# A Mamba block and a mixture of experts on one core: the engine loop written out, and the gate product of y in two halves

## What is computed

```python
u, res = split(layernorm(x) @ W_in);  u = silu(u)
delta = softplus(u @ W_delta + b_delta);  Bm = u @ W_B;  Cm = u @ W_C
h_t = exp(delta_t * A) * h_{t-1} + delta_t * B_t * u_t      # 256 channels, 16 states
y_t = sum_n h_t[n] * C_t[n]
x = x + ((y + u * D) * silu(res)) @ W_out
# experts on layernorm(x): 1 shared and 8 routed, of which each token takes 4
x = x + swiglu_shared + sum_e w_e * swiglu_e
```

## Time and profile before

| | us |
|---|---|
| median of 3 runs | 1539.01 |
| lowest and highest | 1535.20, 1539.65 |
| the profiled execution | 1535.95 |
| its span, first to last instruction | 1534.1 |
| what lies around the span | 1.85 |

### The profile page before, as it was taken

One profiled execution on the slowest core, in us unless ns is written; L12 is line 12 of the kernel. 1 busy time (PEld: TensorE's weight loads), 2 busy tenths in 40 slices (PEclk: granted clock), 3 DMA queues, 4 the chain that ended last, 5 costly groups with the idle time before them and its releaser, 6 DMA issues. The chain is left out here.

```text
span 1534.1 us, 31186 instructions
## 1 busy us (share of the span) xinstructions
PE 1473.8 (96%) x9510; PEld 1245.7 (81%) x9510; DVE 1413.0 (92%) x2834; ACT 1230.3 (80%) x1841; POOL 850.2 (55%) x508
## 2 busy tenths in 40 slices
PE   4879999999999999999999999999999999999998
PEld 3677887888788887888879788887978888898887
DVE  5869999999999999999999999999999999999843
ACT  5978888888789798888979888897988889787331
POOL 5965564665456376555647556564755657375100
PEclk7999999999999999999999999999999999999999
DMA  5320212112111211211121131112202120201000
GB/s 183 95 99 22 74 34 81 43 57 77 35 57 43 90 41 37 95 35 56 42 90 41 36 96 35 56 42 70 87 10 87 46 63 29 98 15 57 1 8 8
DMA packets 50482, 87.02 MB, mean 57 GB/s; under 512 B 4663, under 2 KB 32820, under 8 KB 50356
## 3 DMA queue, kind: packets, MB, share of 16 engines
q1 hardware_dynamic: 49556, 82.52, 16.6%
q10 hardware_dynamic: 800, 3.14, 0.6%
HBM read 80.93 MB, written 4.72 MB: 56 GB/s over the span
## 5 line engine op out<-in xcount | busy, mean ns | idle before, releaser
L641 POOL TENSOR_TENSOR hb<-soft,bbc 128x1024 f32<-128x1024 f32 x256 | 628.2, 2479 | 21.4 <-DMA bbc<-b_rows 18.3
L1131 PEld LDWEIGHTS eo_bank<-w_sb,gated 128*128 128x128 f32 x3840 | 470.5, 192 | 30.6 <-issue 17.5
L1131 PE MATMUL eo_bank<-w_sb,gated 128*128 128x128 f32 x3840 | 488.2, 276 | 2.7 <-DVE o L937 1.9
L861 DVE SCALAR_TENSOR_TENSOR acc<-turn,c_sb,acc 128x256 f32<-128x256 f32 x900 | 375.9, 474 | 13.3 <-issue 10.6
L696 ACT ACT_TABLE_LOAD x299 | 383.6, 1283 | 5.4
L849 DVE TENSOR_TENSOR_SCAN hb<-decay_bank,hb 128x512 f32<-128x512 f32 x256 | 310.7, 1214 | 24.3 <-POOL hb L641 14.1
L1064 PE MATMUL turn<-ident,hb 128*128 128x128 f32 x2048 | 291.6, 275 | 36.1 <-DVE hb L849 16.9
L794 ACT ACTIVATE s<-h 128x512 f32<-128x512 f32 x384 | 221.8, 598 | 126.8 <-PE h L1115 121.0
L849 DVE TENSOR_TENSOR_SCAN hb<-decay,hb 128x512 f32<-128x512 f32 x256 | 318.3, 1274 | 2.0 <-ACT decay L776 1.8
L1064 PEld LDWEIGHTS turn<-ident,hb 128*128 128x128 f32 x2048 | 241.9, 142 | 82.8 <-issue 22.5
L928 DVE TENSOR_TENSOR gated<-h,s 128x512 f32<-128x512 f32 x384 | 253.5, 678 | 28.0 <-PE h L1115 17.6
(11 more groups left out here) (105 smaller groups left out, 1511.2 us busy)
## 6 DMA issues: line engine op xcount, KB each, us to landing
bbc<-b_rows SPq DMA_DIRECT2D x128, 512.0 KB, 5.1
x_in<-x_dram SPq DMA_DIRECT2D x16, 256.0 KB, 3.0
x_cur<-x_dram SPq DMA_DIRECT2D x16, 256.0 KB, 6.3
out_dram<-o SPq DMA_DIRECT2D x15, 256.0 KB, 2.5
gated<-w_all_dram ACTq DMA_DIRECT2D x1, 1534.5 KB, 8.6
hb<-w_all_dram ACTq DMA_DIRECT2D x1, 1534.5 KB, 12.4
w_sb<-w_all_dram SPq DMA_DIRECT2D x5, 192.0 KB
b_rows<-cbT SPq DMA_DIRECT2D x16, 32.0 KB, 1.6
```

Of the source, the lines that this page charges most:

```text
L641: pool.tensor_tensor(hb[:, arg % HB_RING, :, :], du[:, h, :].unsqueeze(1).broadcast_to((P, GN, TOK)), bbc[:, r, :].rearrange("p (n t) -> p ...
L861: dve.scalar_tensor_tensor(acc[:, blk, :], turn_bank[pair][:, i * DI:(i + 1) * DI], c_sb[:, blk, n:n + 1], acc[:, blk, :], ALU.mult, ALU.add)\
L1131: mm = pe.matmul(eo_bank[:, blk * P:(blk + 1) * P], gated[:, k % GATED_RING, blk * P:(blk + 1) * P], w3_sb[:, pair, :], start=(n == 0), st ...
```

## The change

`bodies` no longer makes a run-time loop. It writes the nine passes out, with j put in as a number, so that head, passes and tail are one straight list for each engine. Everything that dealt with the seams goes: the branch, the registers, the `side_free` ahead of the loop, and ACT's look at which function table the loop expects. On POOL, `ymul` is made in two halves of 128x512, the first after `z.0`, the second after `z.1`; `y_ready` now counts two a tile. The order of steps is the same on every engine.

```diff
         def bodies(eng, engine, program):
             head, body, tail = ORDER[engine]
-            program([((tile, 0), step, arg) for tile, step, arg in head], None)
-            with eng.Fori(*LOOP) as j:
-                program([((j, SHIFT[part]), step, arg) for part, step, arg in body], body)
-            program([((tile, 0), step, arg) for tile, step, arg in tail], body)
+            program([((tile, 0), step, arg) for tile, step, arg in head]
+                    + [((j + SHIFT[part], 0), step, arg) for j in range(*LOOP) for part, step, arg in body]
+                    + [((tile, 0), step, arg) for tile, step, arg in tail])
...
                     elif step == "ymul":
-                        pool.wait_ge(z_ready, count(turn, NH, NH))
                         pool.wait_ge(sres_ready, count(turn, NH, NH))
-                        pool.tensor_tensor(y[:, :, :], y[:, :, :], sres[:, :, :], ALU.mult).then_inc(y_ready, 1)
+                        for h in range(NH):
+                            pool.wait_ge(z_ready, count(turn, NH, h + 1))
+                            pool.tensor_tensor(y[:, h, :], y[:, h, :], sres[:, h, :], ALU.mult).then_inc(y_ready, 1)
...
-            def program(entries, before):
-                table = table_after(before, None) if before else EXP_TABLE
-                head = before is None
+            def program(entries):
+                table = EXP_TABLE
...
                     elif step == "wi_res":
-                        wait_before(act, y_ready, turn, 1, 0)
+                        wait_before(act, y_ready, turn, NH, 0)
...
-                wanted = table_after(ORDER["act"][1], None)
-                if head and table != wanted:
-                    act.preload_act_table_set(wanted)
...
-            def program(entries, before):
-                if before is None:
-                    last = None
-                elif isinstance(entries[0][0][0], int):
-                    last = last_side(before, lambda part: (LOOP[1] - 1, SHIFT[part]))
-                else:
-                    side_free(last_side(ORDER["pe"][0], lambda tile: (tile, 0)))
-                    last = last_side(before, lambda part: (entries[0][0][0], SHIFT[part] - 1))
+            def program(entries):
+                last = None
...
                     elif step == "wo":
-                        pe.wait_ge(y_ready, count(turn, 1, 1))
+                        pe.wait_ge(y_ready, count(turn, NH, NH))
```

More of the change, by code:

```diff
@@ L975, in side_free @@
                     wait_before(pe, reader, turn, per, GATE_STEPS if step == "gate" else arg + 1)
-            def last_side(entries, turn_of):
-                uses = [(turn_of(at), step, arg) for at, step, arg in entries if step in SIDE]
-                return uses[-1]
             def stay_busy(times):
```

## The result

| | us |
|---|---|
| median after, 6 runs | 1548.06 (1544.80 to 1550.02) |
| median before, 6 runs | 1537.57 (1535.20 to 1540.35) |
| ratio | 1.0064, 95% interval 1.0047 to 1.0082 |
| profiled execution after, and its span | 1549.70, 1547.6 |

The changed kernel is 0.6% slower, where 0.9% faster was forecast. A time of 1525.7 us was expected, within 1520.5 to 1531.5.

A forecast was written before the change was run, and what follows sets the result against it. PE was taken as the bound, about 88.6 us a tile. Gains of 10.3 (branches), 3.0 (entry wait) and 0.3 less 0.3 (`ymul` halves) made 13.3 us: 1525.7 against a median of 1539.01, range 1520.5 to 1531.5.

The forecast's parts named there:

- The bound: PE in the loop's passes: about 88.6 us of its own work a tile; DVE's work 0.8 us a pass below.
- The eight branches: Taken branches at the loop's end: removing them and DVE's gap after each gains 10.3 us, between 8.8 and 10.6.
- The wait ahead of the loop: `side_free` at loop entry, holding PE before `turn.6`: removing it gains 3.0 us, between 2.27 and 3.03.
- Fetching: Instruction fetch in the nine written-out passes: 45 more packets on q8, costed at nothing.
- the slower rival: PE starves in the straight list, up to 1.27 us idle per new q8 packet: 1583 us; chance 0.04.
- `ymul` in halves: POOL's gate product of y: first half falls into POOL's 4.08 us idle time before `z.1`; sum 0.
- two small terms: `ymul` halves: 0.3 us lost in tile 0 (1.9 if a half takes 2.11), 0.3 gained in tile 15.
- the gap is given back by other waits: Loop passes settle at 89.3 us as PE meets DVE or ACT elsewhere: 7.5 us gained, 1531.5; chance 0.10.

The follow-up runs named there:

- written-out loop alone: Against the changed kernel: loop still written out, but POOL's gate product of y is one 128x1024 instruction after both z, as before; 1522.19 us, ratio 0.9895.
- both halves behind z.1: Against the changed kernel: both halves of POOL's gate product wait for z.1, so no POOL work runs between z.0 and z.1; 1524.49 us, ratio 0.9904.
- added instruction, one input: Against the added product kernel: the extra POOL instruction behind z.0 reads one operand, a scale of y half 0, instead of two; 1526.08 us, ratio 0.9924.
- added product: Against the written-out loop alone: one more 128x512 POOL product after z.0, into a tile nobody reads; 1533.23 us, ratio 0.9975.
- second half alone: Against the written-out loop alone: only channels 128 to 255 of the gate product are multiplied, after z.1; 1534.54 us, ratio 0.9978.

## Why the prediction was wrong, step by step

**The bound.** The number was right: the forecast of 88.66 us a pass, taken from the one pass that no branch preceded, was met with 88.49, PE without a gap. The reading, that PE is the bound and DVE has 0.8 us a pass to spare, was not. Eight passes in six kernels with the loop written out, us:

| kernel | eight passes | DVE busy in them | difference |
|---|---|---|---|
| written-out loop alone | 707.94 | 700.47 | 7.47 |
| both halves behind z.1 | 709.46 | 701.89 | 7.57 |
| added instruction, one input | 711.02 | 703.50 | 7.52 |
| added product | 716.18 | 708.71 | 7.47 |
| second half alone | 717.64 | 710.25 | 7.39 |
| changed kernel | 726.14 | 718.53 | 7.61 |

Whatever DVE gets more to do, the passes get longer by, to within 0.2 us, and from the first 0.2 us a pass on. So DVE had no slack in the written-out loop: the 0.93 us a pass in which it isn't busy stay in every kernel. In part of them it waits for PE (3.9 us in eight passes of the written-out loop alone), so it may be the two together that set the pace; the rest isn't resolved. Nor is a full row of PE proof that PE sets the pace: with both halves behind `z.1` it is busy for 709.36 of 709.46 us, with the same products as in 707.94.

**The eight branches.** Right in kind and nearly in size: 10.3 us were forecast. In the kernel with DVE alone written out the eight passes take 719.56 - 708.08 = 11.5 us less, 0.9 over the 10.6 that was called the upper bound.

**The wait ahead of the loop.** Right: 3.0 forecast; the stretch ahead of the passes is 3.1 us shorter where this wait alone was taken out, 3.2 in the written-out loop alone and 3.3 in the changed kernel. Where it is shorter still, 85.9 us with both halves behind `z.1`, a meeting is missing that the kernel before has there: a scan at 376.6 us that started behind a `dbu` and took 3.28 us, with PE waiting 1.4 us for `gated` after it. So the kernel before pays for such meetings too.

**Fetching.** Right: the 1583 us of the slower rival have no trace; PE is busy for all of 707.94 us on a straight list, in which 38 packets came on q8.

**`ymul` in halves.** This step failed, with the slack that it leant on. The prediction said of the first half that it "falls into that idle time", that the change "is cover, not time", and of `dbu.4` that it "starts 1.1 us earlier" and "no one waits for that". By the semaphores all of this holds; it leaves out that a POOL instruction and a scan can make each other stand still. It priced the step at 0, with 1.9 us at most for tile 0; it costs 25.9. (Its two small terms came about as forecast: in tile 0 PE waits 4.2 us for y in place of 4.0, and the 0.31 us in tile 15 are gone.) What POOL's idle time was worth was read from POOL's row, where idle time of an engine that isn't the bound costs nothing. It should have been read from what DVE did in those 4.08 us: two scans that need POOL silent. And it took 0.8 us of slack a pass as enough for DVE "to follow" without asking what could lengthen DVE's work. The scans of a pass grew by 2.3 us. With 0.8 us of slack a pass would have come to 90.0; there was none, and it took 90.8.

The trace of before had the evidence, unread. Of its 256 scans from `decay`, 27 took more than 1.25 us, up to 3.32, and each of these had started while a POOL instruction ran and ended 1.08 or 1.09 us after it; the scan at 737.78 is one of them. POOL's sums at L666 took 1.26 to 2.11 us, a spread that I kept as an uncertainty of the price and didn't explain: the 12 that had started during such a scan took 1.69 to 2.11, the 18 others 1.26 to 1.31. The Trainium skill states the mechanism (SBUF — State Buffer, SBUF: two separate sides): a DVE instruction with two SBUF inputs and a GpSimd instruction that reads SBUF contend for a shared pair of ports; whichever starts first has it as an exclusive lock for the whole instruction, and the other is fully blocked. The traces agree, but for 0.13 us of overlap at the seam: every blocked scan ends 1.07 to 1.09 us after its blocker, where alone it takes 1.21. It was the rule that spoke against this change, and it wasn't weighed.

**The rivals.** None of them was this one. The one called "the gap is given back by other waits" named PE waiting for `gated` at up to 89.3 us a pass; that is how half of the loss shows on PE (6.8 us, beside the 6.4 ahead of `ct`), but by a DVE that has more work, not by an order that doesn't fit, and it was priced below what came.

What stays open: the gain of the run without the entry wait was nearly twice what its trace shows, and what lowers the granted clock in some executions is not known, nor how much of their 5 us of variation comes from it.

## What to carry to other kernels

Before work is moved on POOL, list the DVE instructions with two SBUF inputs that will run beside it, and count each meeting as the remaining time of whichever came first, here less 0.13 us (1.16 us left and 1.03 lost in the first meeting); an operand in PSUM takes an instruction off that list. Idle time of one engine can be what lets another run, so ask of every gap what the neighbours do in it. Where a run-time loop leaves an "issue" gap after each taken branch, writing out the one engine that has it gave here all but 0.1 us of what writing out all five gave in eight passes.

## What the runs showed of the hardware

- A DVE scan of 128x512 with both inputs in SBUF takes 1.21 us alone. Started while a POOL instruction with one or two SBUF inputs runs, it ends 1.07 to 1.09 us after that instruction does (shown above: five cases, 1.57 to 2.59 us long). The same scan with one input in PSUM takes 1.21 us, and never more than 1.23 in the 256 cases of the kernel before, 211 of which started while POOL was at work.
- It works both ways: a POOL product of 128x512 that takes 1.28 us took 2.06 when it started 0.22 us after such a scan, and a POOL instruction with one input took 1.36 in place of 0.62. The profile counts the blocked time as busy on either engine.
- After a taken branch DVE's next instruction came 3.3 us later, where ACT's came after 0.2 us. Written out, DVE had no gap, and the packets on the instruction queues left no mark on any engine. Between 485 and 1200 us of the changed kernel these were 37 on q8 and 36 on q14, where the kernel before had none on q8 and 49 on q14.
